# Spreading the expert gates over the partitions: by DMA through DRAM instead of by TensorE, from row 2 on

## The reference, cut to what matters

```python
xn = layer_norm(x) * gamma + beta
logits = einsum('bsd,de->bse', xn, Wr) + br           # 8 experts
top_vals, top_idx = top_k(logits, 2)
w = softmax(top_vals)
w_full = einsum('bsk,bske->bse', w, one_hot(top_idx, 8))
for e in range(8):                                    # every expert on every token
    h = gelu(einsum('bsd,dh->bsh', xn, W1[e]) + b1[e])
    y = y + (einsum('bsh,hd->bsd', h, W2[e]) + b2[e]) * w_full[..., e, None]
```

## Time and profile before

| | |
|---|---|
| device time, median of 3 | 407.26 us (407.03 to 407.29) |
| the profiled execution | 406.67 us |
| its span, first to last instruction | 404.7 us |
| PE busy | 382.7 us (95%) |
| DVE busy | 346.8 us (86%) |
| ACT busy | 331.8 us (82%) |
| POOL busy | 259.6 us (64%) |
| granted PE clock | 0.997 of full |
| spread matmuls (`hid_lo,sel`) | 62, of which 46 for units 16 to 61 |

### The profile page before, as it was taken

How to read it: one execution, slowest core, us unless ns; L and a number is a source line. 1 busy time by engine, 2 the same in 40 slices (tenths; PEclk the granted TensorE clock), 3 DMA queues, 4 the chain that set the end, 5 groups by cost and what they waited for, 6 DMA issues and landing times.

```text
span 404.7 us, 6382 instructions
## 1 busy us (share of the span) xinstructions
PE 382.7 (95%) x1980; PEld 310.7 (77%) x1980; DVE 346.8 (86%) x825; ACT 331.8 (82%) x618; POOL 259.6 (64%) x382
## 2 busy tenths in 40 slices
PE   4999799999999999999999999999998999999995
PEld 2787578888888888888888878778776877786774
DVE  3897879888888988988888889999977899899886
ACT  1688989989999998988977855687887998997982
POOL 0686997787778788778777557586322664454451
PEclk9999999999999999999999999999999999999998
DMA  5900022122122121223312000000000000000001
GB/s 188 385 5 0 2 52 38 42 52 50 32 54 52 26 55 43 46 44 52 47 34 52 2 0 2 0 2 2 1 0 2 1 2 13 14 15 13 15 13 26
DMA packets 15849, 14.93 MB, mean 37 GB/s; under 512 B 9797, under 2 KB 10569, under 8 KB 15561
## 3 DMA queue, kind: packets, MB, share of 16 engines
q1 hardware_dynamic: 15816, 14.54, 14.4%
HBM read 13.42 MB, written 1.11 MB: 36 GB/s over the span
## 4 chain that ended last, share of the span: by engine, by line
PE 64%; DVE 16%; ACT 8%; issue 5%; POOL 3%; DMA 2%; SPq 1%; DVEq 0%; ACTq 0%
PE ps L1566 58%; PE ps L1589 4%; ACT w_all L919 2%; DVE hid L1432 1%; ACT x L913 1%; ACT hid L913 1%; DVE hh L1328 1%; DVE kstat L1268 1%; DVE x L1284 1%; DVE x L1432 1%; DMA xn<-in_w_f 1%; DMA rstd_row<-roots 1%; DVE qmax L1280 1%; DVE qsum L1294 1%; PE ps L1770 1%
## 5 line engine op out<-in xcount | busy, mean ns | idle before, releaser
L1113 DVE TENSOR_TENSOR hid_lo<-hid,hid_hi 128x1024 fp32r<-128x1024 f32 x64 | 78.9, 1233 | 25.2 <-ACT hid_hi L751 25.1
L746 ACT ACTIVATE hid<-ps,b_fold 128x512 f32<-128x512 f32 x128 | 83.8, 682 | 18.7 <-PE ps L1566 18.3
L1566 PE MATMUL ps<-xn_hi,w_all 128*128 128x512 f32 x256 | 88.3, 404 | 1.3 <-DVE xn_lo L1108 1.3
L1566 PE MATMUL ps<-hid_hi,w_all 128*128 128x512 f32 x256 | 85.0, 393 | 0.0
L751 ACT ACTIVATE hid_hi<-hid 128x1024 fp32r<-128x1024 f32 x64 | 67.9, 1061 | 2.0
L1566 PEld LDWEIGHTS ps<-xn_hi,w_all 128*128 128x128 f32 x256 | 48.4, 189 | 12.4 <-DVE xn_lo L1108 2.7
L1566 PEld LDWEIGHTS ps<-hid_hi,w_all 128*128 128x128 f32 x256 | 48.0, 188 | 9.9
L1566 PE MATMUL ps<-xn_lo,w_all 128*128 128x512 f32 x128 | 49.9, 390 | 0.0
L1566 PE MATMUL ps<-hid_lo,w_all 128*128 128x512 f32 x128 | 49.8, 389 | 0.0
L1566 PE MATMUL ps<-hid_hi,ew 128*128 128x512 f32 x131 | 41.2, 400 | 0.7 <-ACT memT L855 0.4
L537 POOL TENSOR_TENSOR var_in<-var_in 128x4 f32<-128x4 f32 x32 | 36.5, 1142 | 2.6
(11 more groups left out here) (232 smaller groups left out, 920.0 us busy)
## 6 DMA issues: line engine op xcount, KB each, us to landing
rstd_row<-roots SPq DMA_DIRECT2D x29, 256.0 KB, 3.8
hh<-in_tokens SPq DMA_DIRECT2D x8, 256.0 KB, 7.8
hid<-in_w SPq DMA_DIRECT2D x1, 1024.0 KB, 7.5
rstd_row<-in_w SPq DMA_DIRECT2D x1, 1024.0 KB, 9.8
out<-hh SPq DMA_DIRECT2D x7, 128.0 KB, 2.0
ew_raw<-in_expert_w SPq DMA_DIRECT2D x1, 512.0 KB, 9.1
roots<-rstd SPq DMA_DIRECT2D x29, 2.0 KB, 1.4
ew_raw<-in_expert_w SPq DMA_DIRECT2D x1, 256.0 KB, 9.2
```

The source lines that it names most:

```text
L746: act.activation(hid[:, j % 2, f, :], bank[f], ACT.Gelu, bias=b1_fold[:, j // B * F + f:j // B * F + f + 1]).then_inc(gelu_done, 1)
L1113: dve.tensor_tensor(hid_lo[:, j % 2, 2 * p:2 * p + 2, :], hid[:, j % 2, 2 * p:2 * p + 2, :], hid_hi[:, j % 2, 2 * p:2 * p + 2, :].bitcast( ...
L1566: return pe.matmul(out, lhsT, rhs, start=start, stop=stop)
```

## The change

Units 16 to 61 (`BY_DMA = 2 * E` on) get their gates in another way; units 0 to 15 stay as they are.

1. DVE writes each group's gates once more, halved, in token order (`gates_tok`), one tensor_scalar per group at the end of `gates_out`.
2. SP stores them to DRAM, one DMA per row, in runs of 4 floats (16 bytes).
3. For each unit SP loads the unit's 512 gates from DRAM to all 128 partitions (256 KB), into one of four slots of `rstd_row`. The load of unit n waits until unit n-4 is multiplied.
4. PE's spread matmul for these units is gone. The PE wait `h1_ready` stands at unit 16 still.
5. DVE multiplies by the slot in SBUF, where the gates lie in (partition, tile) order, so they are read with a step of 4 floats (16 bytes). It waits for `gates_loaded`, and for the second products of the unit that used the `hw` buffer six units before (`multiplied`, or `y_done` at a row's end).
6. SP's output stores now stand between the loads, at the sixth unit of a row.

```diff
+BY_DMA = 2 * E
+GROUPS_ROWS = ((0, 1, 2, 3), (4, 5), (6, 7))
...
+def spread_by_dma(n):
+    return n >= BY_DMA and not alone(n)
...
+        gates_hbm = nc.dram_tensor("gates_rows", (B, E, S), fp32).ap()
+        gates_tok = sb("gates_tok", [P, B, E, NT])
+        gate_spread = rstd_row
...
+            def store_gates(p):
+                sp.wait_ge(gates_split, p + 1)
+                for b in GROUPS_ROWS[p]:
+                    sp.dma_start(gates_hbm[b].rearrange("e (p t) -> p e t", t=NT),
+                                 gates_tok[:, b, :, :]).then_inc(gates_stored, 16)
+
+            def load_gates(n):
+                b, e = divmod(n, E)
+                if n == BY_DMA:
+                    sp.wait_ge(ctx_done, B)
+                if n >= BY_DMA + 4:
+                    sp.wait_ge(hw_ready, gated(n - 3))
+                sp.wait_ge(gates_stored, 16 * (GROUPS_ROWS[GROUP_OF[b]][-1] + 1))
+                sp.dma_start(gate_spread[:, n % 4, :], gates_hbm[b, e].partition_broadcast(P)).then_inc(gates_loaded[n % 4], 16)
...
+            store_gates(0)
+            for n in range(BY_DMA, UNITS):
+                m, u = divmod(n, E)
+                if u == 5:
+                    store_output(m - 2)
+                if n == 3 * E + 4:
+                    store_gates(1)
+                if n == 6 * E - 1:
+                    store_gates(2)
+                if spread_by_dma(n):
+                    load_gates(n)
...
+                dve.tensor_scalar(gates_tok[:, rows[0]:rows[-1] + 1, :, :],
+                                  wgt[:, r, :].rearrange("p (b t) e -> p b e t", t=NT),
+                                  0.5, None, ALU.mult).then_inc(gates_split, 1)
...
             def dve_job(n):
                 slot = n % NSLOT
                 dve.wait_ge(eg_done, n + 1)
+                if spread_by_dma(n):
+                    dve.wait_ge(gates_loaded[n % 4], 16 * loaded(n))
+                    if ends_row(n - NSLOT):
+                        dve.wait_ge(y_done, (n - NSLOT) // E + 1)
+                    else:
+                        dve.wait_ge(multiplied, not_last(n - NSLOT))
+                    dve.tensor_tensor(hw(slot).rearrange("p (t q) -> p t q", t=NT),
+                                      hg(n % NHG).rearrange("p (t q) -> p t q", t=NT),
+                                      gate_spread[:, n % 4, :].rearrange("p (q t) -> p t q", t=NT),
+                                      ALU.mult).then_inc(hw_ready, 1)
+                    return
                 dve.wait_ge(wb_done, gated(n + 1))
                 dve.tensor_tensor(hw(slot), hg(n % NHG), bank[spread_bank(n)],
                                   ALU.mult).then_inc(hw_ready, 1)
...
-                    if not alone(n):
+                    if n == 2 * E:
+                        pe.wait_ge(h1_ready, B)
+                    if n < BY_DMA:
                         spread_gates(n)
```

More of the change, by code:

```diff
@@ L166, in lo_by_dve, with not_last, loaded @@
     return split(n) and (n % E in LO_BY_DVE or n == UNITS - 3)
+def spread_by_dma(n):
+    return n >= BY_DMA and not alone(n)
+def not_last(n):
+    return sum(not alone(k) and not ends_row(k) for k in range(n + 1))
+def loaded(n):
+    return sum(spread_by_dma(k) for k in range(n % 4, n + 1, 4))
 def ends_row(n):
@@ L420, in build @@
         hw_ready, hwhi_act = sem("hw_ready"), sem("hwhi_act")
+        gates_split, gates_stored, multiplied = sem("gates_split"), sem("gates_stored"), sem("multiplied")
+        gates_loaded = [sem("gates_loaded%d" % k) for k in range(4)]
         alone_done, alone_taken = sem("alone_done"), sem("alone_taken")
@@ L492, in _, with store_output @@
                 sp.dma_start(rstd_row[:, slot, :], roots_hbm[slot].partition_broadcast(P)).then_inc(rstd_loaded, 16)
-            for b in range(B):
+            def store_gates(p):
[11 more added lines that the diff above has]
+                sp.dma_start(gate_spread[:, n % 4, :], gates_hbm[b, e].partition_broadcast(P)).then_inc(gates_loaded[n % 4], 16)
+            def store_output(b):
                 dst = out_hbm[b, :, :].rearrange("(t p) c -> p t c", p=P)
@@ L499, in _ @@
                     sp.dma_start(dst[:, t, :], tiles(h1[:, b, :])[:, t, :]).then_inc(stored[(b + k) % 2], 16)
+            store_gates(0)
[9 more added lines that the diff above has]
+                    load_gates(n)
+            store_output(B - 2)
+            store_output(B - 1)
             sp.wait_ge(stored[0], 16 * (B // 2 + 1))
@@ L1425, in gates_out @@
                                   ALU.subtract).then_inc(gates_ready, 1)
+                rows = GROUPS_ROWS[p]
+                dve.tensor_scalar(gates_tok[:, rows[0]:rows[-1] + 1, :, :],
+                                  wgt[:, r, :].rearrange("p (b t) e -> p b e t", t=NT),
+                                  0.5, None, ALU.mult).then_inc(gates_split, 1)
             def dve_job(n):
@@ L1966, in spread_gates @@
                 e = n % E
-                if n == 2 * E:
-                    pe.wait_ge(h1_ready, B)
                 last = last_use(n, spread_bank)
-                if last is not None and n != 2 * E:
+                if last is not None:
                     pe.wait_ge(hw_ready, gated(last + 1))
@@ L1986, in second_products @@
                     pe.wait_ge(hw_ready, gated(n + 1))
-                    mm(bank[6 + b % 2], w2_whole[:, WHOLE_EXPERTS.index(e), :], hw(slot), start=False, stop=False)
+                    mm(bank[6 + b % 2], w2_whole[:, WHOLE_EXPERTS.index(e), :], hw(slot),
+                       start=False, stop=False).then_inc(multiplied, 1)
                     return
@@ L1997, in second_products @@
                     last.then_inc(y_done, 1)
+                else:
+                    last.then_inc(multiplied, 1)
             def turn_sum(b):
```

## The result

The changed kernel takes 437.74 us, median of 4 runs (436.72 to 441.99); the kernel before took 407.27 on the same chip (407.03 to 408.37). The ratio is 1.077 (95% interval 1.074 to 1.080). I had forecast 418.0, range 409.5 to 431: the sign and the first mechanism were right, the size was not, because a second cost that I had put at 0 came on top. The profiled execution of after took 436.72 us, 30.05 more than that of before.

What follows compares the result with a forecast made beforehand. It took PE, ACT and DVE as nearly level before and DVE as full after the change. Holds +11.0, tail -0.8 and stores +0.5 gave +10.7 on 406.67, so 417.4, or 418.0 us as median; range 409.5 to 431.

Steps and rivals of the forecast that it cites:

- The bound: Multiply 16 to 61: PE, ACT, DVE nearly level; removing 46 matmuls gains at most 0.3 us per plain row.
- The multiply alone: DVE's gate multiply: moving its second input from PSUM to SBUF leaves the instruction's own time the same, cost 0.
- The holds: DVE multiplies and POOL low parts, reading SBUF, exclude each other: 1.1 us per POOL instruction, +11.0 us in all.
- POOL asks for its turn while a multiply runs and gets it right after: POOL's low parts beside a full DVE: each waits for one running multiply only; part of the 1.1 us price.
- The step: DVE's multiply reading gates 4 floats apart: taken at 0, with bounds of 0 and +10.6 us.
- Rival D: The step doubles the multiply's gate read: 0.53 us each, +24.3 in all, 442.3 us; chance 12%.
- C: Rival: the step costs 0.23 us per multiply on top of the forecast, 428.6 us; chance 10%.
- The slack: DVE's idle time, 1.8 us per plain row, absorbs part of the added 3.6 us per row.
- Stores: Gate stores in 16-byte pieces ahead of loads 28 and 47: 0.25 us each, 0.5 in all.
- rival E: Small-piece stores hold up loads 28 and 47 by several us: +5 to +15 on the forecast; chance 5%.
- The loads, the copies, `multiplied`: Loads land in 3.8 us and barely fit; gate copies take 0.22 each; the new wait for products costs 0.
- The tail: Program's end: output follows the last low part without DVE's 0.72 us wait for PE's transposes: -0.8 us.

Runs made afterwards that it cites:

- u1: Kernel before without spread matmuls, gate loads or stores from unit 16 on; the multiply reads a stale PSUM bank: 406.11 us, ratio 0.999 to the kernel before.
- b1: u1 with the multiply's second input read from an old SBUF slot, without a step: 419.61 us, ratio 1.029 to the kernel before.
- b2: b1 with the 16-byte step on the multiply's second input, still no DMA of gates: 437.56 us, ratio 1.075 to the kernel before.
- a1: Changed kernel with all loads and stores, but the multiply reads its slot without the 16-byte step: 422.89 us, ratio 1.038 to the kernel before.
- c1: b1 with POOL's low part replaced by three fills that only write the same tile: 404.52 us, ratio 0.994 to the kernel before.
- s1: b1 with eight forms of the multiply in turn, with different steps and operand places, run for their durations: 425.34 us in one execution.
- a8: a1 with all eight rows' gate stores issued at the first group's time, none at units 28 and 47: 419.57 us, ratio 1.030 to the kernel before.
- c2: Changed kernel with the 46 spread matmuls put back as filler into an unread PSUM bank: 437.38 us, ratio 1.075 to the kernel before.

## Why the prediction was wrong

Where the 437.7 comes from, by differences of medians: 406.1 (u1) + 13.5 (second input in SBUF, b1) + 18.0 (step, b2 less b1) + 0.2 (DMA of the gates, after less b2). By the other way round it is + 3.3 (DMA, a1 less b1) + 14.8 (step, after less a1). The prices depend on what is there already, and the four executions of b2 lie 5.4 us apart, so these runs don't settle whether the DMA costs after 0 or 3 us.

- **The bound: right.** DVE carries the loss. The removed matmuls are worth nothing measurable; I had 0.3 us per plain row. The granted clock of PE fell, which I had named as a sign of being wrong (0.67 to 0.98 in the windows of after). But b1 has its loss in five rows at a clock of 1.00, and the plain row of after has DVE full at 0.98.
- **The multiply alone: right for the move, wrong for the read.** From SBUF in plain order it takes 0.68, as the earlier trace rows said.
- **The holds: right.** "So the two engines exclude each other, whoever is first", 1.1 us a hold: b1 has just this. Of the windows I forecast +11.0, b1 has +10.1, and row by row it comes within 0.6 us but for the first and the last, where I was 1.1 and 1.3 too high. One of these I could have counted: the trace before has three POOL low parts in the first window, not four, since unit 19 has none. Of its total I forecast 407.3 + 11.0 - 0.8 = 417.5 and it took 419.6; the difference lies in the tail, with PE at a granted clock of 0.50. The Trainium skill (SBUF — State Buffer, "Who interferes with whom") says that a GpSimd instruction is in the way of a DVE instruction with two SBUF inputs if it reads SBUF, and not if it only writes it. The trace agrees: in c1, where POOL only writes, no multiply is over 0.69. Its full hold gave an estimate of +15.6, more than the b1 stretch shows.
- **"POOL asks for its turn while a multiply runs and gets it right after": half right.** Mostly it does. With stepped multiplies back to back it stood for 4.15, 4.58 and, in b2, 7.19 us. This is a cost of the two together that the prediction has no term for.
- **The step: the failed step.** "So what PE can fetch at this step is enough for DVE: I take 0." It costs 1.07 - 0.68 = 0.39 us each, and 14.8 in all (after less a1). I had two rows of another engine that disagreed, the long records of the weight loads and the short time of four transposes, and took the second to speak for DVE. They spoke for PE. Rival D, whose mechanism this is (priced at 0.53 each, 442.3 us), had 12%, and C (0.23 each, 428.6) 10%; the truth lies between. The Trainium skill (Advanced Engine Details and Errata, "SBUF Cachelines") says that two accesses to a 16-byte line are enough and one is penalised. The runs agree: with two (a step of 8 bytes) a multiply takes 0.68, with one (16 bytes) 1.07. That a step of 32 bytes is hardly worse is from s1 alone.
- **The slack: counted right for one cost.** I subtracted DVE's idle time once, and b1 has 1.7 us of it left. The step on top of the holds costs 18.0 in b2, as much as its full price (46 x 0.39 = 17.9), though part of that is waiting behind POOL; where it is alone it costs 11.3.
- **Stores: 0.5 forecast, 3.3 measured without the step.** The mechanism is rival E's, at less than its 5 us, and my bounds held it; I went by the 1.4 us that 128 pieces take, and two stores of 1024 take 5.6. How much of the 3.3 is left in after is open.
- **The loads, the copies, `multiplied`: right.** a8 equals b1; the copies of gates take 0.21 to 0.27; in after no multiply waits for PE (in c2 one does, 2.5 us).
- **The tail: wrong, -0.8 forecast.** The wait has another cause than the spread matmuls: u1 has none of these and waits 0.81. In after it is gone, but DVE is later by its own hold, and the tail is 0.8 longer.

The terms sum up along one way: 418.0 + 14.8 (step) + 2.8 (stores) + 2.1 (b1 over its forecast) = 437.7. The error is in the main one unmeasured price, and the range left out the dearer of the two rivals that had it. Open is which rule gives POOL its turn, what the stores cost in after, and what after would take at a full PE clock.

## What to carry to other kernels

Before an operand moves to another memory, ask two things of the trace: who else reads from there at the same time, and with what step it will be read. Where the only evidence for a price comes from another engine, keep the whole span of it in the range, and put a kernel with that one instruction at the head of the runs. Slack is spent once: two costs on the same engine must be added before the idle time is taken off, and on an engine that others wait for, the sum can cost more than itself.
